# A new order of work on each engine in the attention strips of a fused convolution, attention and MLP block

## The reference, cut to what matters

```python
x = relu(bn(conv1x1(relu(bn(conv3x3_grouped(relu(bn(conv1x1(x)))))))) + x)
shortcut = x
y = layernorm(x) * norm1_w + norm1_b
win = windows(roll(y, (-3, -3)))                 # 2048 windows of 49 tokens
q, k, v = split(win @ qkv_w.T)                   # 8 heads of 16
attn = softmax(q @ k.T * scale + bias + mask)
out = (attn @ v) @ proj_w.T + proj_b
x = shortcut + roll(unwindow(out), (3, 3))
z = layernorm(x) * norm2_w + norm2_b
return x + gelu(z @ fc1_w.T + fc1_b) @ fc2_w.T + fc2_b
```

## Time and profile before

| | |
|---|---|
| median of 3 runs | 4877.54 us (4868.76 to 4878.87) |
| the profiled execution | 4880.38 us, of which the span of instructions is 4878.6 us |
| PE busy | 4590.0 us (94%) |
| PE weight loads busy | 3230.5 us (66%) |
| DVE busy | 3646.7 us (75%) |
| ACT busy | 3537.4 us (73%) |
| POOL busy | 2552.6 us (52%) |
| PE's granted clock, 1000 to 4000 us | 1.00 of full speed |

### The profile page before, as it was taken

The page is one execution under the profiler, slowest core; times in us unless marked ns, Lnnn a source line. Parts: engine busy times, 40 slices in busy tenths (PEclk is TensorE's granted clock), DMA queues, the critical chain, the costliest instruction groups (busy, mean ns, idle before and its releaser), DMA issues.

```text
span 4878.6 us, 192818 instructions
## 1 busy us (share of the span) xinstructions
PE 4590.0 (94%) x71190; PEld 3230.5 (66%) x71190; DVE 3646.7 (75%) x7461; ACT 3537.4 (73%) x5899; POOL 2552.6 (52%) x3498
## 2 busy tenths in 40 slices
PE   8999996999999999999999999999999999999998
PEld 5666664666666666666666666666666666666665
DVE  4343435888888888888888888888888888888886
ACT  3344444778778777877877877877787787787786
POOL 4344433555555555555555555555555555555554
PEclk9999998999999999999999999999999999999999
DMA  4445441100000100100100000010010010000000
GB/s 134 153 145 158 144 136 39 28 26 27 26 26 26 28 26 26 28 27 26 28 27 26 27 28 27 26 28 26 26 28 27 26 28 27 27 27 26 26 26 24
DMA packets 298299, 218.70 MB, mean 45 GB/s; under 512 B 43247, under 2 KB 245486, under 8 KB 298158
## 3 DMA queue, kind: packets, MB, share of 16 engines
q1 hardware_dynamic: 294632, 215.41, 15.1%
q10 hardware_dynamic: 3526, 1.12, 0.1%
HBM read 110.78 MB, written 111.94 MB: 46 GB/s over the span
## 4 chain that ended last, share of the span: by engine, by line
PE 64%; DVE 19%; issue 11%; ACT 5%; DVEq 1%; POOL 0%; DMA 0%; ACTq 0%; POOLq 0%
DVE xn L1084 9%; PE bank L577 8%; PE bank L658 7%; PE bank L633 6%; PE bank L502 6%; PE bank L569 5%; DVE sc L1059 5%; PE bank L600 5%; PE bank L515 4%; PE bank L649 4%; PE bank L560 3%; PE bank L587 3%; DVE z L1084 3%; ACT L862 2%; PE bank L480 2%
## 5 line engine op out<-in xcount | busy, mean ns | idle before, releaser
L1084 DVE SCALAR_TENSOR_TENSOR xn<-x,lnp 98x128 f32<-98x128 f32 x1024 | 874.0, 912 | 3.7 <-POOL lnp L1154 3.7
L1218 POOL TENSOR_TENSOR res<-x,projb 98x512 f32<-98x512 f32 x256 | 325.8, 1273 | 1013.9 <-DVE x L1101 1013.9
L1236 POOL TENSOR_TENSOR sc<-sc,mx 128x784 f32<-128x784 f32 x512 | 788.6, 1540 | 57.2 <-DVE mx L1065 57.2
L658 PE MATMUL bank<-g,fc_sb 128*128 128x392 f32 x2048 | 784.6, 506 | 0.2
L1059 DVE TENSOR_TENSOR sc<-bank,shared 128x392 f32<-128x392 f32 x1024 | 529.7, 560 | 310.5 <-PE bank L587 310.5
L862 ACT ACTIVATE g<-bank,fc1b 128x392 f32<-128x392 f32 x1024 | 574.1, 586 | 125.8 <-PE bank L651 112.5
L649 PE MATMUL bank<-zt_hi,fc_hi 128*128 128x392 f32 x1024 | 453.8, 443 | 153.1 <-ACT g L862 147.7
L600 PE MATMUL bank<-ident_sb,sc 128*113 128x128 f32 x4096 | 530.9, 273 | 0.3 <-ACT shared L872 0.2
L1154 POOL TENSOR_TENSOR lnp<-st 98x8 f32<-98x8 f32 x777 | 145.8, 216 | 731.6 <-DVE st L927 728.0
L600 PEld LDWEIGHTS bank<-ident_sb,sc 128*113 128x113 f32 x4096 | 515.6, 177 | 3.0 <-ACT shared L872 0.7
L1065 DVE TENSOR_REDUCE mx<-sc 128x16 f32<-128x784 f32 x512 | 496.7, 970 | 18.4
(11 more groups left out here) (106 smaller groups left out, 9187.0 us busy)
## 6 DMA issues: line engine op xcount, KB each, us to landing
x<-x_scratch SPq DMA_DIRECT2D x768, 49.0 KB
out_x<-y SPq DMA_DIRECT2D x672, 49.0 KB
xc_even<-in_x SPq DMA_DIRECT2D x128, 196.0 KB
shared<-in_x SPq DMA_DIRECT2D x128, 196.0 KB
x_scratch<-xc_even SPq DMA_DIRECT2D x128, 196.0 KB
x_scratch<-shared SPq DMA_DIRECT2D x128, 196.0 KB
x<-x_scratch SPq DMA_DIRECT2D x256, 38.5 KB
out_x<-y SPq DMA_DIRECT2D x224, 38.5 KB
```

The costliest lines, as they stand in the source:

```text
L658: mm = nc.tensor.matmul(RC[:, 0:ST], fc2[:, c, :], g[:, c], start=c == 0, stop=c == HC - 1)
L1084: ins = V.scalar_tensor_tensor(dst[:, p, :], src[:, p, :], lnp[:, 7, i, p:p + 1], lnp[:, 8, i, p:p + 1].to_broadcast([PT, C]), ALU.add, AL ...
L1236: P.tensor_tensor(out=s_r, in0=s_r, in1=m_r.to_broadcast([128, 2 * HEADS, N]), op=ALU.subtract).then_inc(sub_done, 1)
```

## The change

Only the order within `strips` on PE, ACT and DVE is changed, and one eviction moves from ACT to DVE.

- PE: z is transposed first. K is projected ahead of V (both halves together), then Q. The first two transposes of probabilities come directly behind; then two hidden parts, both halves of the scores, two hidden parts, two transposes of probabilities, both halves of the MLP output, the row sums and both halves of the attention.
- ACT: `zt_out`, `k_out`, `v_out`, then the gelu table is loaded by a written-out instruction, then `pt_out` 0 and 1, then the four gelus, `pt_out` 2 and 3, the other table, `exponentials(t, 0)`, `yt_out` and only then `reciprocals`.
- DVE: `x1_stats` is first; then `zt_rest`, `v_out`, `q_out` (new here), both norms, and behind them bias and maxima.
- POOL and SP are as they were.

```diff
--- before.py
+++ after.py
@@ -573,8 +573,9 @@
 
             def project(t, i):
 
+                part = 1 - i
                 wait(pe, a_out, A_JOBS * t.n + 1 + i)
-                nc.tensor.matmul(RA[:, 0:ST], wqkv[:, C * i:C * i + C], xt[:],
+                nc.tensor.matmul(RA[:, 0:ST], wqkv[:, C * part:C * part + C], xt[:],
                                  start=True, stop=True).then_inc(a_full, 1)
 
             def scores(t, i):
@@ -667,43 +668,36 @@
 
             def strips(t):
                 ahead, t1, t2, t3 = t.back(-1), t.back(1), t.back(2), t.back(3)
-                if t.there():
-                    pe.wait_ge(a_out, A_JOBS * t.n + 1)
-                    project(t, 0)
                 if t3.there():
                     pe.wait_ge(z_sb, t3.n + 1)
                     wait(pe, c_out, C_JOBS * t3.n)
                     to_channels(RC, z, c_full)
                 if t.there():
+                    project(t, 0)
                     values(t, 0)
+                    values(t, 1)
                     project(t, 1)
-                    values(t, 1)
-                if t3.there():
-                    hidden(t3, 0)
-                if t.there():
-                    scores(t, 0)
-                if t3.there():
-                    hidden(t3, 1)
-                if t.there():
-                    scores(t, 1)
-                if t3.there():
-                    hidden(t3, 2)
                 if t1.there():
                     probs_t(t1, 0)
                     probs_t(t1, 1)
                 if t3.there():
+                    hidden(t3, 0)
+                    hidden(t3, 1)
+                if t.there():
+                    scores(t, 0)
+                    scores(t, 1)
+                if t3.there():
+                    hidden(t3, 2)
                     hidden(t3, 3)
                 if t1.there():
                     probs_t(t1, 2)
                     probs_t(t1, 3)
                 if t3.there():
                     mlp_out(t3, 0)
+                    mlp_out(t3, 1)
                 if t1.there():
                     row_sums(t1)
                     attend(t1, 0)
-                if t3.there():
-                    mlp_out(t3, 1)
-                if t1.there():
                     attend(t1, 1)
                 if ahead.there():
                     pe.wait_ge(xn_sb, ahead.n + 1)
@@ -832,12 +826,6 @@
                 nc.scalar.activation(xt[:].rearrange("c w n -> c (w n)"), RA[:, 0:ST], ACT.Identity, scale=ln[:, 0:1],
                                      bias=ln[:, 1:2]).then_inc(a_out, 1)
 
-            def q_out(t):
-                act.wait_ge(a_full, A_JOBS * t.n + 2)
-                wait(act, s_full, t.n)
-                nc.scalar.activation(qt[:, :, 0:N], RA[:, 0:ST].rearrange("c (w n) -> c w n", n=N),
-                                     ACT.Copy).then_inc(a_out, 1)
-
             def v_out(t):
                 act.wait_ge(b_full[0], 4 * t.n - 2 if t.c or not t.fixed else 1)
                 act.wait_ge(vb_clear, 1)
@@ -845,7 +833,8 @@
                     "p (w q d) -> p w q d", w=WINS, q=QUADS), ACT.Copy).then_inc(b_out[0], 1)
 
             def k_out(t):
-                act.wait_ge(a_full, A_JOBS * t.n + 3)
+                act.wait_ge(a_full, A_JOBS * t.n + 2)
+                wait(act, s_full, t.n)
                 for hh in range(2):
                     i = nc.scalar.activation(km[:, :, hh, :], RA[:, 0:ST].rearrange("c (w n) -> c w n", n=N),
                                              ACT.Identity, scale=headmask[:, hh:hh + 1])
@@ -887,21 +876,20 @@
 
             def strips(t):
                 ahead, t1, t2, t3 = t.back(-1), t.back(1), t.back(2), t.back(3)
-                if t.there():
-                    q_out(t)
                 if t3.there():
                     zt_out(t3)
                 if t.there():
                     k_out(t)
                     v_out(t)
                 if t3.there():
-                    gelu(t3, 0)
-                    gelu(t3, 1)
-                    gelu(t3, 2)
+                    nc.scalar.preload_act_table_set("gelu_and_others")
                 if t1.there():
                     pt_out(t1, 0)
                     pt_out(t1, 1)
                 if t3.there():
+                    gelu(t3, 0)
+                    gelu(t3, 1)
+                    gelu(t3, 2)
                     gelu(t3, 3)
                 if t1.there():
                     pt_out(t1, 2)
@@ -910,10 +898,10 @@
                     nc.scalar.preload_act_table_set("natural_log_exp_and_others")
                 if t.there():
                     exponentials(t, 0)
+                if t3.there():
+                    yt_out(t3)
                 if t1.there():
                     reciprocals(t1)
-                if t3.there():
-                    yt_out(t3)
                 if ahead.there():
                     xt_out(ahead)
                 if t.there():
@@ -1040,6 +1028,11 @@
                 V.tensor_copy(vb[0:N, t.u, :, :, 0], RB[0][0:N, :].rearrange(
                     "p (w q d) -> p w q d", w=WINS, q=QUADS)).then_inc(b_out[0], 1)
 
+            def q_out(t):
+                dve.wait_ge(a_full, A_JOBS * t.n + 3)
+                wait(dve, s_full, t.n)
+                V.tensor_copy(qt[:, :, 0:N], RA[:, 0:ST].rearrange("c (w n) -> c w n", n=N)).then_inc(a_out, 1)
+
             def zt_rest(t):
                 dve.wait_ge(c_out, C_JOBS * t.n + 1)
                 V.tensor_tensor(out=zt_lo[:], in0=RC[:, 0:ST], in1=zt_hi[:].bitcast(fp32),
@@ -1113,26 +1106,24 @@
 
             def strips(t):
                 ahead, t1, t2, t3 = t.back(-1), t.back(1), t.back(2), t.back(3)
+                if ahead.there():
+                    x1_stats(ahead)
                 if t3.there():
                     zt_rest(t3)
                 if t.there():
                     v_out(t)
+                    q_out(t)
                 if ahead.there():
-                    x1_stats(ahead)
+                    x1_norm(ahead)
+                if t2.there():
+                    x2_norm(t2)
                 if t.fixed and t.c == 0:
                     bias_and_mask()
                 if t.there():
                     biased(t, 0)
-                if t.there():
                     maxima(t, 0)
-                if t.there():
                     biased(t, 1)
-                if t.there():
                     maxima(t, 1)
-                if ahead.there():
-                    x1_norm(ahead)
-                if t2.there():
-                    x2_norm(t2)
                 if t1.there():
                     ot_out(t1)
                 if t3.there():
```

## The result

The kernel after takes **4935.1 us** (median of 4 runs, 4932.9 to 4938.1) against 4875.1 (4868.8 to 4878.9) before: a ratio of 1.0121, 95% interval 1.0109 to 1.0134. The forecast was 4948, with 4850 to 5020 as its range. The profiled execution of after has a span of 4933.3 us.

What follows compares the result with a forecast made beforehand. PE was taken to bound the kernel before at 15.85 us a strip; the change would close a loop of 16.13 us across engines, +0.28 us over 253 strips, +71 us, giving 4948 us, range 4850 to 5020.

Steps and rivals of the forecast that it cites:

- The bound before: Kernel before: PE sets the period of 15.85 us a strip, 15.15 of it PE's own work.
- (a) the table: PE's stall of 0.58 us a strip ahead of the third MLP product, for ACT's gelu, goes.
- (b) like products: Like products side by side on PE spare six changes of shape a strip, taken as 0.8 us.
- (c): `q_out` leaves ACT and costs DVE about 0.55 us.
- (d) the norms: DVE's norms get out from beside POOL and cost 1.05 us each; DVE sheds 2.28 us.
- The loop: One turn from projection through statistics, POOL's factors, norms, maxima, exponentials, rsum and `ot` to the next projection takes 16.13 us.
- The V eviction: DVE's later `v_out` is a new wait for PE, some 0.8 us a strip at the transposes of probabilities.
- The chain over V: From projection through `v_out`, PE's products, row sums and `ot` to the next projection: 15.4 us, 0.7 shorter than the loop.
- The sum: +0.28 us a strip over 253 strips gives +71 us, so 4948 us, 1.4% slower.
- The filling strips: The few filling and draining strips change by a few us either way, put at 0 with ±5.
- Rival 1: The loop doesn't bind; PE and the V eviction set the period, so faster, down to 4764 us; chance 0.17.
- The loads of x1: SP's loads for the earlier x1 statistics have seven us left, so no cost; an image's last strip has less.

Runs made afterwards that it cites:

- old_dve: The kernel before with the new order on PE and ACT and `q_out` on DVE, DVE's list otherwise as before; 5175.7 us, 6.1% slower than before.
- q_on_act: The kernel after with `q_out` moved back from DVE to ACT, behind `v_out`; 4931.7 us.
- norms_behind: The kernel after with both norms put back behind the last maxima on DVE, x1 statistics still first; 5174.9 us, 4.9% slower than after.
- pool_plus: The kernel after with three more small additions in POOL's factors, results unused; 5068.4 us.
- pe_plus: The kernel after with PE's four transposes of xn made twice; 4937.4 us.
- stats_early_sp_rs: The kernel after with x1 statistics a strip earlier, SP's wrapped-row copies behind the next strip's loads, ACT's reciprocals ahead of `yt`; 4692.7 us, 0.9629 of before.
- stats_early: The kernel after with DVE's x1 statistics made one strip earlier, behind the last maxima, and two more end strips written out; 4881.8 us.
- z_behind_max: The kernel after with only the z norm moved behind the first maxima on DVE; 5051.2 us.
- stats_behind_v: The kernel after with DVE's x1 statistics put back behind `v_out`, norms still ahead of the bias; 5400.1 us.
- before_norms_ahead: The kernel before with only DVE's norms moved ahead of bias and maxima; 5539.3 us, 13.5% slower than before.

## Why the prediction was right, point by point

- **The bound before** was read rightly, but not fully. PE set the period, and DVE's chain through the norms stood right behind it. The 0.12 us that PE waited for `ot` was that chain showing: in the strip of the rows it is 6.98 from projection to bias, 3.92 for bias and maxima (2515.14 - 2511.22) and 5.07 for norms, `ot` and handoff (2520.21 - 2515.14), and so the whole strip. `old_dve` shows how little room it had.
- **(a) the table** and **(b) like products**: the stall of 0.58 went, and PE's own work fell to 16.15 - 1.04 - 0.50 = 14.61, so by 0.54 us, where I took 0.8 (0.6 to 1.1 from six changes of shape). The term was too big by a quarter of a microsecond; since nothing of it was on the path, this cost nothing. That it is changes of shape that were spared, no run shows by itself.
- **(c)** `q_out` at 0.55 us: the row of after says 0.55, hidden in a wait, as `q_on_act` shows.
- **(d) the norms** take 1.14 us for four xn instead of 3.41. Right, and shown by `norms_behind` from the other side.
- **The loop**: 16.13 forecast, 16.12 measured (16.15 from 1000 to 4600 us). The path and the waits were right; that the sum agrees to some 0.02 is luck, for the terms' own bounds were 15.85 to 16.5, and the two turns are 16.05 and 16.24. The largest error of a term is the handoff from rsum to `ot` (0.66 for 0.57). `pool_plus` and `pe_plus` show that it is the loop that counts and that PE's work isn't.
- **The V eviction**: PE's wait for it was put at 0.8 and is 0.50, that for `ot` at 1.0 and is 1.04. The chain over V was called 0.7 shorter than the loop; `stats_early_sp_rs` runs at 15.18 a strip, with the x1 statistics taken out of that chain, so this is not contradicted, but the 15.4 was not measured by itself.
- **The sum**: +71 us for the strips against 69. The filling strips were put at 0 ± 5 and gave 6.5 back: in the old order POOL's factors of the second strip ran beside DVE's building of the bias table, and their first three instructions took 4.68 us instead of 0.54, which is 4.1 of it; in the new order they run ahead of it.

Timeline of the kernel before, POOL, second strip:

```profile
775.72 4.68 POOL L1154 TENSOR_TENSOR lnp<-st 98x8 f32<-98x8 f32 x3 [9.81 <-DVE st L927]
```

- **Rival 1**, the time if the loop didn't bind: the step that speaks against it held. The Trainium skill (Perfetto Trace Analysis, Identifying the Most-Contended Engine) tells one to optimize the engine with the highest occupancy first, and by PE's 94% this change would have been a gain. The page adds, what the prediction left out, that TensorE's headroom is to be judged by the share of its weight loads instead: that is 66%, below DVE's 75% and ACT's 73%, so by that measure it isn't PE that the page names. The runs don't bear out the first reading: `pe_plus` shows that PE, still the highest at 90%, was not the bound any more.
- **The loads of x1** had time enough in after, as said: no wait of DVE for a DMA is among its waits. `stats_early` shows where that ends, in the last strip of an image, which I had named.

What I missed lies in the experiments: the wait of `x2_out` for POOL's `res2` (`z_behind_max`), the later start of the scores in PE's new order (`old_dve`), and PE's low clock behind some of the longer stalls (`stats_behind_v`, `old_dve`, `before_norms_ahead`).

## What to carry to other kernels

When several engines run written-out lists, ask of every reordering which closed loop it makes: follow the semaphores from one turn to the same point of the next, add up start-to-start distances from the rows, and compare the sum with the period; here that gave 16.13 for 16.12. Leave no wait of a loop's instructions out: `z_behind_max` was missed by 293 us for one. An engine's busy share says nothing about such a loop: 0.5 us on POOL, 51% busy, cost 0.5 us a strip, and 0.4 us on PE, 90% busy, cost nothing. Having found the loop, take out of it what doesn't belong there (statistics that could be made a strip earlier, a copy in front of the reciprocals); that turned a loss of 1.2% into a gain of 3.7%.

## What the runs showed of the hardware

- Four norm instructions with two SBUF inputs on DVE take 1.12 to 1.14 us with POOL idle, 2.39 beside one subtraction of POOL, and 3.41 beside two POOL instructions behind each other. POOL's own subtraction takes 1.52 to 1.56 in all of them. The Trainium skill (SBUF — State Buffer, Who interferes with whom) lets whichever starts first keep the shared ports for its whole instruction; that DVE alone loses time in these rows, because POOL is nearly always inside an instruction when DVE asks, agrees with it but isn't a proof. The other way round stands in the filling strips of before: sixteen additions of DVE behind each other, from two SBUF tensors, run from 775.56 to 779.99 us, and POOL's three small instructions that start at 775.72 take 4.68 us instead of 0.54.
- PE's clock fell to its low level for a few microseconds at a time in the kernels where PE waited longer: in `stats_behind_v` after waits of 1.36 and 1.15 us (granted clock 0.53 from 2519 to 2526 us), in `old_dve` after 1.49 and 0.61 (0.60 from 2534.7 to 2539); the projection then took 2.02 instead of 1.11 us. The length of the last waits doesn't settle it. After 1.30 and 1.15 us in `stats_behind_v` (the projection at 2558.17) it took 1.11; after 1.37 and 0.61 us it took 1.79 in `old_dve` (2500.31) and 1.11 in `norms_behind` (2534.37); after one wait of 2.20 us in `before_norms_ahead` it took 1.74 (2537.51), after one of 2.22 it took 1.04 (2501.89). What decides between them stays open. In after, with 0.92 to 1.14 us at the projection and 0.50 at the transposes, the granted clock is 1.00 from 1000 to 4000 us.
- What the low level cost there: a strip that begins with a slow projection takes 19.2 us instead of 17.4 in `stats_behind_v` and 17.9 instead of 16.4 in `old_dve`.
